# Expert tiles of a decoder layer: the gate from one Silu on ScalarE, three waits fewer on TensorE, sums taken two tiles later

## The reference

```python
x = x + attention(layernorm(x), ...)
x = x + xattn(layernorm(x), k, bias, ctx, ctx, 8)       # Toeplitz convolution, gated by ctx
x = x + ffn(layernorm(x), ...)

def ffn(hidden_states, ...):                             # 16 experts, 4 per token, I = 176
    router_logits = x @ gate_w.T
    topk_w, topk_idx = top_k(softmax(router_logits), 4)  # weights are normalised to sum 1
    shared = silu_mul(x @ shared_gate_up.T) @ shared_down.T * sigmoid(x @ shared_gate_vec.T)
    for each expert e:
        h = silu(gu[:, :I]) * gu[:, I:]     with gu = x @ w_gu[e].T
        acc += h @ w_down[e].T * combine[:, e]
    return shared + acc
```

## Time and profile before

| | us |
|---|---|
| median of three executions | 611.7 |
| lowest, highest | 608.62, 612.01 |
| the profiled execution, its own time | 609.71 |
| its span, first to last instruction | 607.9 |
| of it up to the first transpose of the tile stage | 438 |

### The profile page before, as it was taken

The page is one execution under the profiler, slowest core; times in us unless marked ns, Lnnn a source line. Parts: engine busy times, 40 slices in busy tenths (PEclk is TensorE's granted clock), DMA queues, the critical chain, the costliest instruction groups (busy, mean ns, idle before and its releaser), DMA issues.

```text
span 607.9 us, 18533 instructions
## 1 busy us (share of the span) xinstructions
PE 575.1 (95%) x5887; PEld 466.1 (77%) x5887; DVE 479.1 (79%) x1454; ACT 413.0 (68%) x1060; POOL 387.7 (64%) x419
## 2 busy tenths in 40 slices
PE   8889899999999999999999999998899999999991
PEld 3558679888898898888888889876677777777770
DVE  4657788878878688798877776687688899999993
ACT  4876876878768778787686775832266666666661
POOL 1146768879888888878787877776300355555563
PEclk9998999999999999999999999989999999999996
DMA  7826333243243332423222020011444578877853
GB/s 227 295 80 174 92 111 122 80 132 116 92 135 79 114 115 62 148 83 129 90 87 86 14 87 24 32 45 63 146 128 135 175 222 237 235 238 233 243 179 112
DMA packets 55681, 78.99 MB, mean 130 GB/s; under 512 B 7202, under 2 KB 46370, under 8 KB 55588
## 3 DMA queue, kind: packets, MB, share of 16 engines
q1 hardware_dynamic: 37300, 48.56, 26.4%
q0 software_dynamic: 6912, 18.88, 10.2%
q10 hardware_dynamic: 11376, 10.36, 4.9%
HBM read 44.48 MB, written 33.29 MB: 128 GB/s over the span
## 4 chain that ended last, share of the span: by engine, by line
PE 78%; issue 7%; POOL 6%; DVE 4%; ACT 3%; DMA 1%; POOLq 0%; DVEq 0%; ACTq 0%
PE ps L832 12%; PE ps L705 9%; PE ps L597 7%; PE ps L632 6%; PE ps L528 5%; PE ps L727 5%; PE ps L855 4%; PE ps L652 3%; PE ps L585 3%; PE ps L636 3%; PE ps L844 3%; PE ps L821 3%; POOL kv_lo L1577 2%; PE ps L568 2%; PE ps L558 2%
## 5 line engine op out<-in xcount | busy, mean ns | idle before, releaser
L1577 POOL TENSOR_TENSOR kv_lo<-kv,kv_hi 128x512 f16<-128x512 f32 x64 | 80.9, 1265 | 30.2 <-ACT kv_hi L972 29.5
L1643 POOL DMA_INDIRECT toeplitz_lo<-y_slots,slots x44 | 42.5, 965 | 81.0 <-DMA y_slots<-kv 61.6
L832 PE MATMUL ps<-w_gate_up_hi,toeplitz_hi 128*128 x316 | 84.0, 314 | 1.4 <-DVE toeplitz_hi L1482 1.1
L1565 POOL TENSOR_TENSOR kv<-ctx_t_sb,v_t 128x512 f32<-128x512 f32 x60 | 64.9, 1090 | 16.0 <-ACT v_t L962 15.9
L1609 POOL DMA_INDIRECT x_slots<-x_norm,slots x60 | 65.0, 1084 | 15.1 <-issue 14.3
L942 ACT ACTIVATE probs<-ps,row_neg_max 128x128 f32<-128x128 f32 x256 | 71.5, 391 | 0.3 <-DVE row_neg_max L1150 0.3
L597 PEld LDWEIGHTS ps<-v_ones,probs_t 128*128 128x128 f32 x512 | 62.2, 192 | 2.2
L597 PE MATMUL ps<-v_ones,probs_t 128*128 128x17 f32 x512 | 60.7, 256 | 0.0
L1537 POOL TENSOR_TENSOR ln_rstd<-ln_var,minus_half 128x1 f32<-128x1 f32 x48 | 30.3, 632 | 43.1 <-DVE ln_var L1105 43.1
L632 PE MATMUL ps<-kv_hi,toeplitz_hi 128*128 128x128 f16 x256 | 56.7, 221 | 1.3 <-POOL kv_lo L1577 0.7
L632 PE MATMUL ps<-kv_hi,toeplitz_lo 128*128 128x128 f16 x256 | 56.6, 221 | 0.0
(11 more groups left out here) (238 smaller groups left out, 2058.0 us busy)
## 6 DMA issues: line engine op xcount, KB each, us to landing
stage<-in_w_units SPq DMA_DIRECT2D x36, 512.0 KB, 3.7
x_slots<-zeros SPq DMA_DIRECT2D x15, 512.0 KB
toeplitz_hi<-x_slots SPq DMA_DIRECT2D x40, 128.0 KB, 2.8
y_slots<-stage ACTq DMA_DIRECT2D x40, 128.0 KB
y_slots<-kv ACTq DMA_DIRECT2D x39, 128.0 KB
kv_hi<-x_slots SPq DMA_DIRECT2D x20, 128.0 KB
x_slots<-zeros SPq DMA_DIRECT2D x1, 2432.0 KB
kv_lo<-x_slots SPq DMA_DIRECT2D x19, 128.0 KB
```

What stands on the lines that cost most here:

```text
L832: last = nc.tensor.matmul(psum[2 + t % 2][:, 0:2 * INTER], bxT[a][t % 2][:, kc, :], egu[b][:, bass.ds(e, 1), kc, :].rearrange("p a n -> p ...
L1565: nc.gpsimd.tensor_tensor(kv[g % 2][:], cs.broadcast_to([P, SIDE, SIDE, SIDE]), vs.broadcast_to([P, SIDE, SIDE, SIDE]), ALU.mult).then_inc ...
L1577: nc.gpsimd.tensor_tensor(flat(kvh[1][g % 2]), kv[g % 2][:].rearrange("p h j i -> p (h j i)"), flat(kvh[0][g % 2]), ALU.subtract).then_inc ...
L1643: pool.indirect_dma_start(out=yg[n][j], out_offset=None, in_=ybuf[0:(last_tile(row, j) + 1) * P], in_offset=bass.IndirectOffsetOnAxis(ap=s ...
```

## The change

ScalarE applies Silu to the gate directly, scaled by 1/`WS`, and VectorE's product (tanh + 1) * gate is gone; the two remaining products take the scale 1/`WS` each. One Silu on a dummy column stands between the stages. On TensorE three waits are left out: `turn_x(t)` on the low half of x of tile t-2, `gate_up(t)` on inner of tile t-2, and `turn_inner(t)` on the low half of inner of tile t-2. ScalarE's wait for the gated product of tile t-2 becomes a wait for inner of tile t-2. Each sum is due 10 steps behind the last tile instead of 8.

```diff
-        bth = [st[:, 1536 + n * INTER:1536 + (n + 1) * INTER] for n in range(2)]
-        bga = [st[:, 1888 + n * INTER:1888 + (n + 1) * INTER] for n in range(2)]
+        bsg = [st[:, 1536 + n * INTER:1536 + (n + 1) * INTER] for n in range(2)]
+        sink = sb("table_sink", [P, 1])
...
-        t_gu, t_th, t_ga, t_inner = (signal(f"tile_{n}") for n in ("gate_up", "tanh", "gated", "inner"))
+        t_gu, t_sg, t_inner = (signal(f"tile_{n}") for n in ("gate_up", "gate", "inner"))
...
                 pe.wait_ge(s_xg[t % NX], 16 * (t // NX + 1))
-                t_xlo.wait(pe, t - 2)
...
                 t_xlo.wait(pe, t)
-                t_inner.wait(pe, t - 2)
...
                 t_inner.wait(pe, t)
-                t_hlo.wait(pe, t - 2)
...
+            nc.scalar.activation(sink[:], minus_half[:], ACT.Silu)
+
...
-            def gate_th(t):
+            def gate_silu(t):
                 t_gu.wait(act, t)
-                t_ga.wait(act, t - 2)
-                nc.scalar.activation(bth[t % 2], psum[2 + t % 2][:, 0:INTER], ACT.Tanh, scale=0.5 / WS)\
-                    .then_inc(t_th.sem, 1)
+                t_inner.wait(act, t - 2)
+                nc.scalar.activation(bsg[t % 2], psum[2 + t % 2][:, 0:INTER], ACT.Silu, scale=1.0 / WS)\
+                    .then_inc(t_sg.sem, 1)
...
             def gate_tile(t):
-                t_th.wait(dve, t)
-                nc.vector.scalar_tensor_tensor(out=bga[t % 2], in0=bth[t % 2], scalar=1.0,
-                                               in1=psum[2 + t % 2][:, 0:INTER], op0=ALU.add, op1=ALU.mult)\
-                    .then_inc(t_ga.sem, 1)
-                t_ga.wait(dve, t)
+                t_sg.wait(dve, t)
                 t_hT.wait(dve, t - 2)
-                up = psum[2 + t % 2][:, INTER:2 * INTER]
-                nc.vector.scalar_tensor_tensor(out=bhh[t % 2][:, 0:INTER], in0=up, scalar=SILU, in1=bga[t % 2],
-                                               op0=ALU.mult, op1=ALU.mult)
-                nc.vector.scalar_tensor_tensor(out=bhh[t % 2][:, P + 64:INTER + 64], in0=up[:, P:INTER], scalar=SILU,
-                                               in1=bga[t % 2][:, P:INTER], op0=ALU.mult, op1=ALU.mult)                    .then_inc(t_inner.sem, 1)
+                up, sg, h = psum[2 + t % 2][:, INTER:2 * INTER], bsg[t % 2], bhh[t % 2]
+                nc.vector.scalar_tensor_tensor(out=h[:, 0:INTER], in0=up, scalar=1.0 / WS, in1=sg, op0=ALU.mult, op1=ALU.mult)
+                nc.vector.scalar_tensor_tensor(out=h[:, P + 64:INTER + 64], in0=up[:, P:INTER], scalar=1.0 / WS,
+                                               in1=sg[:, P:INTER], op0=ALU.mult, op1=ALU.mult).then_inc(t_inner.sem, 1)
...
 def combine_at(row, j):
-    return last_tile(row, j) + 8
+    return last_tile(row, j) + 10
```

More of the change, by code:

```diff
@@ L1082, in _ @@
             for s in range(TILES + 3):
-                for piece, behind in ((x_hi, 0), (gate_th, 1), (inner_hi_tile, 2), (y_out, 3)):
+                for piece, behind in ((x_hi, 0), (gate_silu, 1), (inner_hi_tile, 2), (y_out, 3)):
                     if 0 <= s - behind < TILES:
```

## The result

The changed kernel took 613.14 us (median of 22 runs, 609.15 to 616.22), the kernel before, timed beside it, 610.3 us (22 runs, 607.23 to 612.54). The ratio is 1.0042, with a 95% interval of 1.0026 to 1.0058: slower by 2.6 us, where 0.9 us less had been forecast, and 0.54 us above the range. By the 1% bound this is no change, but the interval leaves out 1, and the sign was wrong. The profiled execution took 611.97 us.

A forecast was written before the change was run, and what follows sets the result against it. The prediction took a two-tile loop through three engines, 1.94 us a tile, as the bound. Gains of 0.55 us (weights meeting sums) and 0.33 us (first gate) made 0.9: 611.7 became 610.8 us, range 606.0 to 612.6.

The forecast's parts named there:

- The step that failed: Whole kernel: of a span of 607.9 us, the change touches only the tile stage, the 170 us behind 438.
- the term for the table load: ScalarE, waiting 4.1 us for the stage's first transpose: the 1.28 us load hides there, cost 0, 2.8 us to spare.
- the signs named: New profile: alternating 1.88 and 2.01 us tiles, 0.55 us less after 487, hidden table load, Silu 0.32, VectorE 15 us less.
- The loop of two tiles through three engines: Steady tile stage, through ScalarE, VectorE and TensorE: 3.89 us per two tiles binds, above TensorE's two floors of 3.76.
- The meeting of weights and sums: Tile-stage steps where VectorE has both `weigh` and the sums, from 487.08: 0.55 us gained, between 0.2 and 0.6.
- either edit would do nearly all of it: Where `weigh` and sums meet: VectorE's shorter step or the later sums alone would give nearly all of 0.55 us.
- The first gate: Start of the tile stage: without the product, the third `x_lo` starts 0.33 us earlier, between 0 and 0.37.
- the three waits: TensorE's sequencer, 51 ns each: in a steady tile they hide behind the wait for `x_lo`, so dropping them gives 0.
- The sequencer: Rival, gap before `gate_up` on TensorE: fewer waits close it, 4.9 us less, 605.9 us; chance 0.07.
- Silu is not longer: Rival denied here, ScalarE between `x_hi` and `y_out`: Silu at twice the Tanh costs 6.1 us, 616.9; chance 0.05.
- The later sums starve nobody: Rival denied here, GpSimd's gathers: late stores hold up loads, sums and `x_lo`, 0.3 us in 13 rows, 614.8; chance 0.03.

The follow-up runs named there:

- dummy Silu: The kernel before plus one Silu on one column between the stages, every tile still running Tanh: 613.9 us, ratio 1.0072.
- the run with Silu alone: The changed kernel with the three waits on TensorE and the sums' distance of eight tiles put back: 612.72 us, ratio 1.0044.
- the run without Silu: The kernel before with its Tanh gate, without the three waits and with sums ten tiles behind: 609.03 us, ratio 0.9989.
- moved constants: Loads of `skip`, `w_route`, `ecol` and `iota` issued behind weight units 2 to 4: changed kernel 607.94 us, kernel before 609.33 us.
- only `w_route` and `ecol` moved: The changed kernel with only these two loads issued behind weight units 2 to 4, `skip` and `iota` staying ahead: 611.85 us, ratio 1.0032.
- square root: The kernel before plus one square root on one column behind ScalarE's last instruction: 614.43 us, ratio 1.0089.

## Why the prediction was wrong, step by step

**The step that failed** stands in its first sentences: that "the change touches the tile stage alone, the 170 us behind 438". All terms of the sum were taken inside that stage, and its start was carried over as it was. The start came 3.0 us later. That is more than the whole sum of 0.9, and it turned the sign. The same error is in the term for the table load, "0, with 2.8 us to spare": the load of 1.28 us is hidden, as forecast, with 2.6 us of waiting left beside it. But its price lay elsewhere: a program that holds a second set lost 4.2 us (the dummy Silu's 613.9 against 609.71), and nothing of it was left to measure once the four late constants stood behind the units (609.18). None of the rivals had the first stage in it, and none of the signs named would have shown the error: all of them lie in the tile stage, and all came out nearly as said.

The base of the forecast was off as well. 611.7 was the median of three executions; over 22 it is 610.3. With that base the forecast would have been 609.4, and the miss 3.7 us instead of 2.3. That the time lies only 0.54 us above the range is luck.

**What was correct in the tile stage, and what was not.** The loop of two tiles through three engines is unchanged, 3.89 us, and the work taken off VectorE buys nothing in the steady part. The meeting of weights and sums gave 0.5 us (0.55 forecast): the lag between the traces falls from 2.81 us at the tile of 487.08 to 2.33 at that of 493.46. That "either edit would do nearly all of it" was wrong, though: the shorter step of VectorE alone gave 0.49 (the run with Silu alone), the later sums 0.13 (the run without Silu). The first gate gave 0.4 (0.33): the lag goes from 3.02 at the first transposes to 2.63 at the first tile's last matmul. Some 0.2 of this is lost again in small steps between 448 and 470 us. The prediction put the three waits at 0, and this loss goes with them: from the first tile's last matmul to the fourteenth's it is 25.22 to 25.26 us in all eight traces with the waits, and 25.35 to 25.74 in all eight without them. Why TensorE loses time where it waits for less was not found. The lag at the stage's last matmul is 2.30. Net, the stage gave 0.7, within the bounds of 0.2 and 1.0. The moved constants show the same without the disturbance, 0.73 us between the two stages. Over all 16 traces the stage takes 156.43 to 156.89 us where the product on VectorE is gone, and 157.20 to 158.53 where it stands. The medians of the two kernels with moved constants lie 1.4 apart; half of that is not explained.

**The rivals.** The sequencer is not the bound: without the 231 waits the pair of tiles still takes 3.89 us, and the kernel without them, with the later sums and its Tanh, ran at 0.9989. Silu is not longer: 317 ns, where the earlier trace rows have 0.32 us for the Tanh. The Trainium skill (ScalarE: Activation LUTs, Step-by-step: what each stage is for) has one element a cycle for every function; the trace agrees, as far as these two durations tell. The later sums starve nobody: VectorE's waits at the end are 3.8 us.

**Is the price paid in every execution?** The six runs with the dummy Silu took 613.03 to 615.53 us, all above the median of before, but single runs of the changed kernel took 609.15 and 609.37. Such a low time doesn't mean that unit 2 was in time: it was late by 2.7 us in the profile at 609.05 (only `w_route` and `ecol` moved), which had no stretch of the lower clock ahead of 596 us. With one profile of each kernel it isn't shown that every execution pays. The Trainium skill (Runtime: NRT & Kernel Launch, Model-switch cost) has the tables brought to the chip at the first execution of a program, or at the first after a switch to another, and steady executions free of it. The trace agrees in that a second set adds no DMA packet. By that page it would cost a steady execution nothing beyond its load; the measurement decides, and it is 4.2 us.

## What to carry to other kernels

Before an activation function is exchanged, count the table sets of the program, not only the time of the load: compare the two traces from their first microsecond on, even if the edit lies at the end. Keep loads that nobody needs soon, above all single rows that go to all partitions, behind the loads that an engine is waiting for: here that move took the changed kernel from a ratio of 1.0042 to 0.9971, about 4.3 us, and the one before from 1 to 0.9992, which is not clear of noise. Less work on an engine that has time left takes no time off: 15 us less on VectorE between 502 and 590 us gave nothing there, and the gain came from the first gate and the three tiles where VectorE was late.

## What the runs showed of the hardware

- In programs with two sets of activation tables, a row of 672 bytes read to 128 partitions (`iota`) landed 6.9 to 7.9 us after its issue in all six profiles that have it ahead of unit 2; with one set it was 3.4 to 3.6 us (four profiles), with three sets 4.3 and 4.7. It was so with Silu's set and with the square root's, used at 438 us or behind ScalarE's last store issue.
- The second and the third set added no DMA packet to the execution (55681 packets, 78.99 MB), and while the loads were late, the 16 DMA engines were busy for 0.39 of the time instead of 0.66.
- With two sets, the 212 KB of `skip` and `iota` delayed the 512 KB queued behind them by 3.3 us, and through them ScalarE and TensorE; queued behind that unit they delayed nothing that was waited for.
- 4.36 us without work on TensorE were followed by a granted clock of 0.50 from 19.3 to 22.7 us; 3.63 us in another run were not. In the profiled executions the number of such stretches ahead of the tile stage went from none to three; the two slowest kernels (dummy Silu, square root) had three.
- One set holds both Silu and Tanh: after one Silu, 79 tiles of Tanh ran without another load.
